# A four-layer gated transformer kernel: gate rows kept as two stacked parts, each expert stage's result turned by halves, the masked-key matmuls spread over the stage before attention

## What is computed

```python
x = x + tanh(g_xattn[L]) * attention_L(layernorm(x), ctx)
x = x + tanh(g_ffn[L])   * experts_L(layernorm(x))
# experts: gates = renormalised top-k of softmax(x @ router); out = sum_e gates[:, e] * expert_e(x)
# layers 0, 1: silu(x Wg) * (x Wu) @ Wd.   layers 2, 3: act(x W1 + b1) @ W2 + b2 (gelu, relu)
# layer 2 adds the layer-normed x itself to the experts' result
# layer 3's attention: score = where(mask == 0, -10000, score) before its softmax
```

## Time and profile before

| | |
|---|---|
| median of 3 runs (lowest to highest) | 660.68 us (659.87 to 660.93) |
| the profiled execution's own time | 657.71 us |
| its span, first to last instruction | 655.9 us |
| mean granted clock of PE, as a share of full speed | 0.949 |
| busy: PE / DVE / ACT / POOL | 611.8 / 484.3 / 358.9 / 201.1 us |
| expert stages, from the first `up` to the last `down` | about 46 to 133, 234 to 291, 370 to 475, 592 to 650 us |

### The profile page before, as it was taken

How to read it: one execution, slowest core, us unless ns; L and a number is a source line. 1 busy time by engine, 2 the same in 40 slices (tenths; PEclk the granted TensorE clock), 3 DMA queues, 4 the chain that set the end, 5 groups by cost and what they waited for, 6 DMA issues and landing times.

```text
span 655.9 us, 11543 instructions
## 1 busy us (share of the span) xinstructions
PE 611.8 (93%) x3408; PEld 441.0 (67%) x3408; DVE 484.3 (74%) x1247; ACT 358.9 (55%) x634; POOL 201.1 (31%) x454
## 2 busy tenths in 40 slices
PE   8999999898999879988999899999997999989996
PEld 5784788556676547855666548888775777744785
DVE  6666799968676468988653539999869888565796
ACT  6333455425666444535565228888734565623785
POOL 4211646540002113521120106666530000211462
PEclk9987999978999989999999769999997999997899
DMA  9225999010000017810002046777310000003571
GB/s 290 70 87 166 216 205 205 14 48 3 11 20 3 2 33 180 200 33 2 6 4 74 0 153 207 238 243 242 112 32 2 3 27 3 4 0 109 176 245 58
DMA packets 32526, 61.10 MB, mean 93 GB/s; under 512 B 6434, under 2 KB 21314, under 8 KB 32476
## 3 DMA queue, kind: packets, MB, share of 16 engines
...
...
## 4 chain that ended last, share of the span: by engine, by line
PE 78%; DVE 11%; ACT 5%; issue 3%; DMA 1%; POOL 1%; DVEq 0%; SPq 0%; ACTq 0%
PE PS L744 12%; PE PS L745 12%; PE PS L746 12%; PE PS L1004 5%; PE PS L912 4%; PE PS L987 4%; PE PS L588 3%; PE PS L775 3%; PE PS L984 2%; PE PS L1021 2%; ACT pT L1307 2%; PE PS L960 1%; PE PS L809 1%; DVE qst L1660 1%; PE PS L941 1%
## 5 line engine op out<-in xcount | busy, mean ns | idle before, releaser
L479 POOL TENSOR_TENSOR wpair<-ring,ones_col 128x128 fp32r<-128x128 f32 (+1 forms) x150 | 66.7, 444 | 171.4 <-PE PS L746 104.8
L1307 ACT ACTIVATE pT<-PS 128x512 f32<-128x512 f32 x160 | 92.7, 595 | 45.8 <-PE PS L987 37.4
L1601 DVE TENSOR_TENSOR PS<-PS,qst 128x512 f32<-128x512 f32 x134 | 93.2, 696 | 20.7 <-ACT PS L1200 18.3
L1607 DVE TENSOR_TENSOR hid_lo<-PS,hid_hi 128x512 fp32r<-128x512 f32 x150 | 102.4, 683 | 1.7 <-ACT hid_hi L1206 1.3
L1206 ACT ACTIVATE hid_hi<-PS 128x512 fp32r<-128x512 f32 x150 | 89.2, 594 | 19.7 <-DVE PS L1601 19.4
L744 PE MATMUL PS<-xhi,wpair 128*128 128x512 f32 x204 | 85.5, 419 | 0.5 <-DVE PS L1589 0.4
L745 PE MATMUL PS<-xlo,wpair 128*128 128x512 f32 x204 | 83.4, 409 | 0.0
L746 PE MATMUL PS<-xhi,wpair 128*128 128x512 f32 x204 | 83.1, 407 | 0.0
L481 POOL TENSOR_TENSOR wpair<-ring,wpair 128x128 fp32r<-128x128 f32 (+1 forms) x150 | 76.8, 512 | 11.8
L1200 ACT ACTIVATE PS<-PS,ring 128x512 f32<-128x512 f32 x88 | 58.3, 662 | 30.3 <-PE PS L746 29.4
L987 PE MATMUL PS<-qst,kz 128*128 128x256 f32 x256 | 64.6, 337 | 2.9 <-ACT pT L1307 2.9
...
## 6 DMA issues: line engine op xcount, KB each, us to landing
qst<-gates SPq DMA_DIRECT2D x44, 512.0 KB, 4.9
...
ring<-in_mlp SPq DMA_DIRECT2D x48, 128.5 KB, 3.1
...
keys<-qst SPq DMA_DIRECT2D x6, 512.0 KB, 3.6
qst<-kfull SPq DMA_DIRECT2D x96, 4.0 KB
...
```

The source lines that it names most:

```text
L479: pool.tensor_tensor(wpair[:, pair, 0, c], w, ones, ALU.mult).then_inc(M["wstep"], 1)
L1307: act.activation(pT[:, w % 8, :], PS[:, 2 + w % 2, :], ACT.Exp, scale=sc).then_inc(A["p"], 1)
L1601: dve.tensor_tensor(o, src, row, ALU.mult).then_inc(M["hid"], 1)
L1607: dve.tensor_tensor(hid_lo[:, kept, :], PS[:, gate_bank(glu, kept), :], hid_hi[:, kept, :].bitcast(f32), ALU.subtract).then_inc(M["lo"], 1)
```

## The change

**Gate rows in two parts.** The turned rows go to banks 0 and 1 in layers 0 and 1 (`row_bank`), and in layers 2 and 3 they are turned ahead of the products of units 2 and 3. ACT copies each half's high part into rows 0 to 31 of `row_pair`, DVE subtracts for the low part into rows 32 to 63, ACT then copies the full rows for SP. Spread and bias product are fp32r passes over the 64 stacked rows. In layers 2 and 3 ACT's activations of units 2 and 3 move behind these copies. The identity passes of layer 2 come first and start the banks. Filler counts ahead of the turns change from 0, 2, 8, 4 to 0, 2, 6, 6.

**Ends of stages.** ACT scales both halves; `turn_back` turns the first half ahead of the last `down`, the second behind it. Fillers: 8 in layers 0 and 1, none in layer 2. The output is stored in two halves.

**Masked keys.** Of the four groups of matmuls two stand before the layer norm's turns, one behind them, one behind three query projections; two fillers take the place of six there.

**Small things.** Layer 2's keys are saved ahead of the gate rows, from other buffers; the prologue prepares `b2pair` and `pick_one` on DVE with five small operations; constants and biases are given to 64 rows.

```diff
+        row_pair = wqpair[0:2 * EP, :, :]
+        rows_hi, rows_lo = row_pair[0:EP, :, :], row_pair[EP:2 * EP, :, :]
+        b2 = {L: ocomb[0:2 * EP, :, :, :].rearrange("p q h c -> p (q h c)")[:, (L - 2) * P:(L - 1) * P] for L in (2, 3)}
...
+
+        def row_bank(L, hf):
+
+            return hf if L < 2 else 6 + hf
...
+                    save_keys(2)
                 save_gates()
                 first_gates()
                 if L == 1:
-                    save_keys(2)
                     stack_keys(2, range(1))
...
-            sp.wait_ge(x_done, NHALF)
-            sp.dma_start(out, x[:, :, :]).then_inc(stored, 16)
-            sp.wait_ge(stored, 16)
+            for hf in range(NHALF):
+                sp.wait_ge(x_done, hf + 1)
+                sp.dma_start(out[:, 4 * hf:4 * hf + 4, :], x[:, 4 * hf:4 * hf + 4, :]).then_inc(stored, 16)
+            sp.wait_ge(stored, 32)
...
             def turn_rows(L):
                 pe.wait_ge(rt["tab"], L + 1)
                 for i in range(NT):
-                    mm = pe.transpose(PS[0:EP, 6 + i // 4, (i % 4) * P:(i % 4 + 1) * P], wtab[:, i, :], ident)
+                    mm = pe.transpose(PS[0:EP, row_bank(L, i // 4), (i % 4) * P:(i % 4 + 1) * P], wtab[:, i, :], ident)
                     if i % 4 == 3:
                         mm.then_inc(rt["tr"], 1)
+
+            def turn_back(L, hf):
+
+                pe.wait_ge(y_out, NHALF * L + hf + 1)
+                for k in range(4):
+                    i = 4 * hf + k
+                    mm = pe.transpose(PS[:, 2 + hf, k * P:(k + 1) * P], yT[:, i * P:(i + 1) * P], ident)
+                mm.then_inc(y_turned, 1)
 
...
                     hf = kept % 2
                     if first:
                         pe.wait_ge(M["hid"], kept % 2 + 1)
+                        pe.wait_ge(rt["lo"], NHALF * L + hf + 1)
                     else:
                         pe.wait_ge(M["lo"], unit - (1 if glu else 3))
...
                     else:
-                        w = consts[0:EP, C_ID3 + entry:C_ID3 + entry + 1].broadcast_to([EP, P])
-                    pe.matmul(PS[:, gate_bank(glu, kept), :], w, gate_rows[:, hf, :], start=True, stop=True).then_inc(M["spread"], 1)
+                        if first and unit >= 2:
+                            pe.wait_ge(rows_out, NHALF * L + hf + 1)
+                        w = pick_one[:, entry:entry + 1].broadcast_to([2 * EP, P])
+                    pe.matmul(PS[:, gate_bank(glu, kept), :], w, row_pair[:, hf, :], start=True, stop=True).then_inc(M["spread"], 1)
...
-                keep_busy(0, (0, 2, 8, 4)[L])
+                if L == 2:
+                    pe.wait_ge(set_dve, 3)
+                    for hf in range(NHALF):
+                        c = slice(hf * HALF, (hf + 1) * HALF)
+                        pe.matmul(PS[:, hf, :], eye[:, :], xhi[:, c], start=True, stop=False, skip_group_check=True)
+                        pe.matmul(PS[:, hf, :], eye[:, :], xlo[:, c], start=False, stop=False, skip_group_check=True)
+                keep_busy(5 if L == 2 else 4 if L == 3 else 0, (0, 2, 6, 6)[L])
+                turn_rows(L)
                 if not glu:
                     for u in (2, 3):
                         up(u, 1, 1, u % 2)
-                turn_rows(L)
-                pe.wait_ge(rows_out, NHALF * (L + 1))
                 if L == 0:
                     pe.wait_ge(astep, 1)
+                    pe.wait_ge(kv_out, KV_LN + 2)
+                if L == 2:
+                    pe.wait_ge(set_dve, 8)
                 for u in range(2 if glu else KEPT):
                     spread(u, u // 2, u, first=True)
-                if L == 0:
-                    pe.wait_ge(kv_out, KV_LN + 2)
                 for hf in range(NHALF):
-                    mm = pe.matmul(PS[:, hf, :], zerob[:, 0:P], zerob[:, :], start=True, stop=False, skip_group_check=True)
-                    if not glu:
-                        mm = pe.matmul(PS[:, hf, :], b2[L][:, :], gate_rows[:, hf, :], start=False, stop=False,
-                                       skip_group_check=True)
-                    if L == 2:
-                        pe.wait_ge(set_dve, 3)
-                        for part in (xhi, xlo):
-                            mm = pe.matmul(PS[:, hf, :], eye[:, :], part[:, hf * HALF:(hf + 1) * HALF], start=False, stop=False,
-                                           skip_group_check=True)
+                    if glu:
+                        pe.wait_ge(rows_out, NHALF * L + hf + 1)
+                        mm = pe.matmul(PS[:, hf, :], zerob[:, 0:P], zerob[:, :], start=True, stop=False, skip_group_check=True)
+                    else:
+                        for part in range(2):
+                            mm = pe.matmul(PS[:, hf, :], b2pair[L][:, part, :], row_pair[:, hf, :], start=(L == 3 and part == 0),
+                                           stop=False, skip_group_check=True)
                     mm.then_inc(M["y"], 1)
...
+                        if u == 2 * n:
+                            turn_back(L, 0)
                         down(u - 1, (u - 1) // 2, (u - 1) % KEPT)
...
+                        if u == 2 * n - 1:
+                            turn_back(L, 0)
                         down(u, u // 2, u % KEPT)
-                pe.wait_ge(y_out, NHALF * (L + 1))
-                for i in range(NT):
-                    mm = pe.transpose(PS[:, 2 + i // 4, (i % 4) * P:(i % 4 + 1) * P], yT[:, i * P:(i + 1) * P], ident)
-                    if i % 4 == 3:
-                        mm.then_inc(y_turned, 1)
-                if L < 3:
-                    keep_busy(4, 16)
+                turn_back(L, 1)
+                if L < 2:
+                    keep_busy(4, 8)
...
+                if L == 3:
+                    pe.wait_ge(masks_ready, 1)
+                    for b in range(2):
+                        count_masked(b)
                 layer_norm(2 * L, (0,))
                 if L == 3:
-                    pe.wait_ge(A["ue"], B)
-                keep_busy(5, 6)
+                    count_masked(2)
+                    keep_busy(4, 2)
+                else:
+                    keep_busy(5, 6)
                 for a in range(HGRP if L == 2 else HGRP - 1):
                     project_queries(0, a, 2 + a)
+                if L == 3:
+                    count_masked(3)
+                    pe.wait_ge(A["ue"], 3)
                 if L == 2:
...
                         if p == 2:
+                            if L == 3:
+                                pe.wait_ge(A["ue"], B)
                             layer_norm(2 * L, (1,))
...
-                act.wait_ge(rt["tr"], NHALF * (L + 1))
-                act.activation(gate_rows[:, 1, :], PS[0:EP, 7, :], ACT.Copy).then_inc(rows_out, 1)
+                for hf in range(NHALF):
+                    act.wait_ge(rt["tr"], NHALF * L + hf + 1)
+                    act.activation(rows_hi[:, hf, :], PS[0:EP, row_bank(L, hf), :], ACT.Copy).then_inc(rt["hi"], 1)
+                for hf in range(NHALF):
+                    act.wait_ge(rt["lo"], NHALF * L + hf + 1)
+                    act.activation(gate_rows[:, hf, :], PS[0:EP, row_bank(L, hf), :], ACT.Copy).then_inc(rows_out, 1)
                 for u in range(2 * RING):
-                    if u >= early:
-                        unit(u, u // 2, u % KEPT)
+                    if u >= 2:
+                        unit(u, u // 2, u % KEPT, first=(u < KEPT))
                     if u > 0:
                         first_part(u - 1, (u - 1) % KEPT, first=(u - 1 < KEPT))
...
                 act.wait_ge(M["y"], UP_AHEAD + 2 * n - 1)
                 act.activation(yT[:, 0:HALF], PS[:, 0, :], ACT.Copy, scale=gtan[:, 4 + L:5 + L]).then_inc(y_out, 1)
+                act.wait_ge(M["y"], UP_AHEAD + 2 * n)
+                act.activation(yT[:, HALF:N], PS[:, 1, :], ACT.Copy, scale=gtan[:, 4 + L:5 + L]).then_inc(y_out, 1)
...
                 layer_norm(2 * L, (0,))
+                if L == 3:
+                    take_masked(2)
                 for a in range(HGRP):
+                    if L == 3 and a == HGRP - 1:
+                        take_masked(3)
                     take_queries(0, a, 2 + a)
...
                 dve.tensor_copy(eye[:, :], ident).then_inc(set_dve, 1)
+                for L in (2, 3):
+                    dve.tensor_copy(b2pair[L][:, 0, :], b2[L]).then_inc(set_dve, 1)
+                    dve.wait_ge(set_dve, 2 * L)
+                    dve.tensor_tensor(b2pair[L][:, 1, :], b2[L], b2pair[L][:, 0, :].bitcast(f32),
+                                      ALU.subtract).then_inc(set_dve, 1)
+                dve.tensor_copy(pick_one[:, :], consts[0:2 * EP, C_ID3:C_ID3 + EP]).then_inc(set_dve, 1)
...
-                dve.wait_ge(rt["tr"], NHALF * L + 1)
-                dve.tensor_copy(gate_rows[:, 0, :], PS[0:EP, 6, :]).then_inc(rows_out, 1)
+                for hf in range(NHALF):
+                    dve.wait_ge(rt["hi"], NHALF * L + hf + 1)
```

(4 more changed lines are left out.)

63 lines of the change are left out of this document (33 added, 30 removed).

## The result

The changed kernel takes 635.59 us, median of 4 runs (631.71 to 636.15), where the kernel before takes 660.63 (659.87 to 660.93): 0.961 of the time, with a 95% interval of 0.957 to 0.965. Forecast were 634.2 us and a range of 628 to 646. The profiled execution took 635.81 us, against 657.71 of the one before. That pair differs by 21.9 us and the medians by 25.0: the execution profiled before was a short one for its kernel (later executions lie between 656.6 and 667.2).

The account below looks back on a forecast made before the run. The prediction took PE as the bound, 78% of the chain. Its terms, 4.0 + 1.5 + 7.5 + 5.8 + 2.9 + 2.0 + 2.8 + 0 = 26.5 us, taken from the median 660.68, gave 634.2 us, range 628 to 646.

Parts of the forecast that it names:

- What bounds the kernel: Whole kernel: TensorE (PE) is 78% of the chain, so only time when PE works or waits counts.
- Layer 2 and 3 starts, 7.5 and 5.8: Expert stage starts, layers 2 and 3: cheaper spreads and bias passes, then ring and gate waits; gains 7.5 and 5.8 us.
- Layer 0's start, 4.0: Expert stage start, layer 0: shorter spreads bring the first down product earlier, gates not later; gain 4.0 us, bounds 2.6 to 5.5.
- Layer 1's start, 1.5: Expert stage start, layer 1: first down product at 247.4 instead of 248.97; gain 1.5 us, bounds 0 and 1.6.
- Ends: Expert stage ends, layers 0, 1, 2: first half turned before the last down product; gains 2.9, 2.0 and 2.8 us.
- the case of the full clock: End of layer 0: the 8 fillers end at 136.6 at full clock, gain 4.0 us.
- the case that I had at 2.3: End of layer 0: the 8 fillers end at 138.4 at half clock, gain 2.3 us.
- the masked keys: End of layer 2: two groups ahead of the turns, not four; with fewer fillers, projections at 482.6 instead of 486.52.
- Layer 3's end, 0: End of layer 3: last add 0.5 us later, halved last store 0.5 back; net 0, plus or minus 0.5.
- The five small operations, nothing: Prologue: five small DVE operations, some 0.7 us, fit in 0.90 us of DVE idle before its first MAX8; cost nothing.
- The slower clock, 0.20: Rival: each start and end has 10 us of half clock; 9.7 us less gain, 644 us; chance 0.20.
- The sum: All starts and ends of the four layers together: 26.5 us gained.

Follow-up runs that it names:

- second profile: The changed kernel, unedited, run and profiled once more as reference: 634.93 us, 0.963 of the kernel before.
- early refills: Changed kernel with, in layers 1 to 3, the ring's first refill ahead of the gate rows' save and the second ahead of gate loads: 639.42 us, 0.969 of before.

## Why the prediction was right, and where it was not

- **What bounds the kernel.** Right. Chain shares, spreads at 0.31 and the vanished half clock agree, and putting float32 back in layers 2 and 3 alone costs 11 us of the 25.
- **Layer 2 and 3 starts, 7.5 and 5.8.** Right in mechanism and in size: 8.2 and 5.5, counted from DVE's table (7.2 and 4.5 by the turns, the shifted landmark). The restart went from PE to ring and gates, as forecast: the `up` of entry 4 starts at 381.41, and its weight from the ring landed 4.50 us after its issue. Forecast were waits of 1 to 2.5 us; they are 1.0 in layer 2 and 1.1 in layer 3, and eight passes more were hidden. In layer 3 the loop from first down product to scaling takes 1.0 longer than before (41.8 for 40.8), by these waits.
- **Layer 0's start, 4.0: the step that failed.** The sentences were "The steady loops between them are bound by PE passes and are not edited", by which an earlier start is a gain to the end, and "Gates are not later". The start itself gained as much as I said or more: row turns to first down product fell from 13.9 to 7.8 us (9.7 in the second profile). But the loop behind it grew from 62.9 to 68.1 us (66.1). What I left out is that in the kernel before the DMA engines are already full behind it (its windows; the DMA share is last but one):

```profile
68.00:91.60 23.60, 23.60 (x104) 19.54 (x105) 20.46 (x33) 12.29 (x22) 13.36 (x26) 1.00 0.95 213
91.60:115.20 23.60, 23.60 (x105) 19.54 (x105) 22.22 (x36) 12.79 (x23) 13.95 (x27) 1.00 0.98 203
```

  PE just kept pace with the bytes there. And the bytes did not come earlier: the first gate load goes out at 61.02 us (60.20 before) and the first refill of the ring at 63.48 (62.69), behind the keys and the rows' save, while the first down product moved from 67.93 to 62.31. So starting earlier moved PE into a wait of 2.6 to 4.0 us for weights. The run with a quarter of the gate bytes shows it: 4.0 us come back.
- **Layer 1's start, 1.5.** Measured 1.0. Row turns to first down product fell by 1.4, as forecast, and the loop behind it took 0.4 longer (40.6 for 40.1).
- **Ends.** 2.0 and 2.8 were met, 2.9 became 3.8, which is the case of the full clock that I had priced at 4.0. In runs where half clock lies on that end it takes 7.6 to 7.9 us instead of 6.1, which is the case that I had at 2.3; I can't say what decides it, since two kernels whose layer 0 is unedited (float32 rows in layers 2 and 3; early refills) show it. As reasons, though, the sizes were wrong. I gave the gain to the turn ahead of the last product, and that is at most 1.0 and 1.1, in layer 2 1.5 with the fillers; the rest is waiting for one's own half only, and the clock. For the masked keys the forecast had the projections 3.9 us earlier because PE "no longer runs 16 fillers and four groups of masked-key matmuls" ahead of the turns: the groups' share is 0.3, because the last group stands ahead of the first scores. The two sums of 2.0 and 2.8 hold all the same: from the first scaling to the projections layer 2's end takes 8.1 us for 11.8 (3.7 less, forecast 3.9); what I had wrong is how they divide.
- **Layer 3's end, 0.** Measured -0.1, but by two parts that were both forecast at 0.5 and cancel: the later last product costs 1.2 to 1.4, and the halved store, together with each half waiting for itself only, gives 1.1 to 1.3 (5.5 and 5.3 us without the turns ahead, 6.6 before). That they cancel is luck. The cost is avoidable.
- **The five small operations, nothing.** I said 0.7 us inside 0.90 of idle time. They take 2.6, and the first MAX8 moved from 22.87 to 24.24:

```profile
21.77 0.65 DVE L1524 CAST b2pair<-ocomb 64x128 fp32r<-64x128 f32 x1
22.45 0.83 DVE L1526 TENSOR_TENSOR b2pair<-ocomb,b2pair 64x128 fp32r<-64x128 f32 x1
...
23.66 0.56 DVE L1526 TENSOR_TENSOR b2pair<-ocomb,b2pair 64x128 fp32r<-64x128 f32 x1
...
24.24 0.42 DVE L1532 MAX8 pT<-PS 128x8 f32<-128x256 f32 x1
```

  Most of it is absorbed before layer 0, where the row turns are 0.5 later (0.0 to 0.7 in the other profiles).
- **The slower clock, 0.20.** It did not come; the clock rose. Its ground was right, though. The Trainium skill, "TensorE: Matmul & The Clock Gate", section "What's actually happening", says that activity releases the throttle, and the run without fillers agrees, with 62 us of half clock and 4 us lost. By that rule alone an engine that is wholly busy would keep its clock; the run with float32 rows in layers 2 and 3 shows 0.57 at 8.00 busy of 8.00 us, so here the measurement decides.
- **The sum.** Terms of 26.5 against 21.9 in the pair of profiles; 3.1 of the gap is layer 0, and 1.8 attention 1. The medians differ by 25.0. The 3.1 us between that and the pair are covered by no term: the terms were read off an execution 3.0 us shorter than the median of its kernel, and I took that scatter for a constant factor. By chance this stands in for what layer 0 lacks, so that the time was met within 1.4 us is luck in part.
